# Two heads to a quarter of the weighing's output, and the last two chunks' experts chosen from the first token's value row

## The reference

```
x = x + 0.5 * ffn(layernorm(x))          # silu gate, two gelu layers, 512 wide, ternary weights with scales
x = x + linear_attention(layernorm(x))
x = x + 0.5 * ffn(layernorm(x))          # the same weights
x = x + 0.5 * experts(layernorm(x))      # 8 experts of rank 64, 2 chosen per sequence
x = x + attention(layernorm(x))          # 16 heads of 8, rotary positions, causal, softmax
x = x + 0.5 * experts(layernorm(x))
```

## Time and profile before

| | |
|---|---|
| median of 3 runs | 667.73 us (667.33 to 671.45) |
| the profiled execution | 668.1 us, span 666.3 us |
| PE busy | 631.2 us (95%) |
| PEld busy | 475.8 us (71%) |
| DVE busy | 495.0 us (74%) |
| ACT busy | 495.1 us (74%) |
| POOL busy | 298.8 us (45%) |
| PE in the chain that ended last | 66% |
| DVE in it | 17% |
| ACT in it | 9% |

### The profile page before, as it was taken

How to read it: one execution, slowest core, us unless ns; L and a number is a source line. 1 busy time by engine, 2 the same in 40 slices (tenths; PEclk the granted TensorE clock), 3 DMA queues, 4 the chain that set the end, 5 groups by cost and what they waited for, 6 DMA issues and landing times.

```text
span 666.3 us, 14363 instructions
## 1 busy us (share of the span) xinstructions
PE 631.2 (95%) x5343; PEld 475.8 (71%) x5343; DVE 495.0 (74%) x1300; ACT 495.1 (74%) x846; POOL 298.8 (45%) x461
## 2 busy tenths in 40 slices
PE   4899999999999999999999999989999999999995
PEld 3587878888887878887778887655555666666664
DVE  6767566585586686686798667999898898888655
ACT  5799688788888788787788677337777777777870
POOL 1402111330331535231574563767878745655661
PEclk9999999999999999999999999989999999999999
DMA  9200000000000002000011144442434322221001
GB/s 301 89 0 1 1 0 1 1 0 1 1 0 1 0 18 79 1 1 1 0 49 48 49 139 177 143 144 78 144 123 137 95 93 94 74 72 40 20 9 41
DMA packets 41886, 37.80 MB, mean 57 GB/s; under 512 B 2940, under 2 KB 37020, under 8 KB 41816
## 3 DMA queue, kind: packets, MB, share of 16 engines
q1 hardware_dynamic: 41816, 36.87, 17.6%
HBM read 21.92 MB, written 14.68 MB: 55 GB/s over the span
## 4 chain that ended last, share of the span: by engine, by line
PE 66%; DVE 17%; ACT 9%; issue 5%; POOL 1%; DMA 0%; DVEq 0%; ACTq 0%; POOLq 0%
PE PSA L940 19%; PE PSA L944 19%; PE PSA L1142 6%; DVE MX L1334 5%; PE PSA L959 3%; DVE G L1206 3%; PE PSA L1095 2%; PE PSA L1129 2%; PE PSA L1079 2%; ACT PSA L1380 2%; PE PSA L1072 2%; PE PSA L1151 1%; ACT G L1376 1%; DVE RA L1327 1%; PE PSA L1102 1%
## 5 line engine op out<-in xcount | busy, mean ns | idle before, releaser
L940 PE MATMUL PSA<-ah,WH 128*128 128x512 f32 x320 | 130.0, 406 | 1.5 <-DVE al L1211 0.9
L1334 DVE TENSOR_REDUCE MX<-PSA 128x6 f32<-128x768 f32 x128 | 118.3, 949 | 15.7 <-PE PSA L1102 15.1
L1380 ACT ACTIVATE PSA<-PSA,SC 128x512 f32<-128x512 f32 x128 | 84.7, 662 | 55.0 <-PE PSA L944 54.3
L944 PE MATMUL PSA<-al,WH 128*128 128x512 f32 x320 | 125.2, 391 | 0.0
L1469 ACT ACTIVATE PB<-PSA 128x768 f32<-128x768 f32 x128 | 99.0, 813 | 17.9 <-PE PSA L1129 16.8
L940 PE MATMUL PSA<-bh,WH 128*128 128x512 f32 x256 | 104.8, 409 | 2.7 <-DVE G L1206 2.3
L1552 POOL TENSOR_SCALAR_AFFINE_SELECT PB<-PB 128x512 f32<-128x512 f32 x128 | 79.5, 635 | 51.7 <-ACT PB L1469 50.3
L944 PE MATMUL PSA<-bl,WH 128*128 128x512 f32 x256 | 100.3, 392 | 0.0
L1498 POOL TENSOR_SCALAR VE<-MV 128x4 f32<-128x4 f32 x46 | 10.9, 236 | 194.7 <-DVE MV L1181 194.7
L1211 DVE TENSOR_TENSOR al<-PSA,ah 128x512 fp32r<-128x512 f32 x64 | 44.0, 687 | 52.6 <-ACT ah L1387 52.2
L940 PEld LDWEIGHTS PSA<-ah,WH 128*128 128x128 f32 x320 | 60.2, 188 | 14.8 <-DVE al L1211 2.2
(11 more groups left out here) (148 smaller groups left out, 1321.0 us busy)
## 6 DMA issues: line engine op xcount, KB each, us to landing
KS<-dk SPq DMA_DIRECT2D x32, 192.0 KB
QS<-dq SPq DMA_DIRECT2D x32, 192.0 KB
dk<-CB SPq DMA_DIRECT2D x16, 192.0 KB, 2.3
dq<-CB SPq DMA_DIRECT2D x16, 192.0 KB, 2.3
VA<-in_ones SPq DMA_DIRECT2D x5, 512.0 KB, 4.4
X<-in_x SPq DMA_DIRECT2D x8, 256.0 KB, 6.9
dk<-CB SPq DMA_DIRECT2D x16, 128.0 KB, 1.9
dq<-CB SPq DMA_DIRECT2D x16, 128.0 KB, 1.9
```

What stands on the lines that cost most here:

```text
L940: e.matmul(o, WH[:, col:col + 128], hi, start=first, stop=False)
L944: return e.matmul(o, WH[:, col:col + 128], low, start=False, stop=last)
L1334: e.tensor_reduce(MX[:, u % 2, 1:4, :].rearrange("p t (l g) -> p l t g", l=2)[:, :, :, g], PSA[:, b:b + 2, 0:384].rearrange("p l (t k) -> ...
L1380: e.activation(bank(b), bank(b), ACT.Gelu, scale=SC[:, k:k + 1]).then_inc(a_gelu, 1)
```

## The change

It has two parts, and the planner's costs and priorities are written anew with them.

**Two heads to a quarter.** A head's tile in VA now has 32 columns of which 16 are its own: 8 of values, 8 of ones, and zeros in the other 16. Heads come in pairs, and a second head's columns are the other 16. The first four heads (`weigh`, g even) and the next four (`weighed`, g odd) go into the same bank, the second adding to the first, so that a quarter holds two heads. The bank is held from the one to the other. ScalarE copies it once, after the second; OT has two parts and not four. One `upright` step of four transposes puts the whole unit into a bank, with one reciprocal of 32 sums and one product of 128x256. The heads are ordered anew in the weights, and the table of ones has zeros in it.

**Experts chosen ahead.** For chunks 6 and 7 a new job, `lone`, follows `prepare` once both feed-forward streams are done. It takes the value row of the first token of both units (`lone`), multiplies it by the output weights and adds the token as it stands in X (`lone_x`), subtracts the mean (`lone_m`), and computes logits and the sum of squares (`lone_g`); VectorE picks the two largest of each unit; GpSimd takes the inverse root (`lone_power`), VectorE scales the difference (`lone_df`), and `tanh`, `gate`, `pick` and `pick_b` follow as for the other chunks, the picks not before the second pass of eight (chunk 6) or ten (chunk 7) units. `half_logit`, `half_tanh` and `half_pick` are gone; `half_expert` waits for its own transposed tokens and for GpSimd's sums. The last two chunks' `proj` waits in the planner until `lone_x` has read the token.

The rest: a unit's `peak` waits in the planner until the one before has sent its maxima; the weighing has priority 6.5; what is left out below are waits, counts of semaphores and names of tiles.

```diff
-TILES = {"pass1": "h", "pass2": "h", "weigh": "q"}
+TILES = {"pass1": "h", "pass2": "h", "weigh": "q", "weighed": "q", "max_out": "q"}
...
-WEIGH = 5.9
+WEIGH = 6.5
...
+LONE = 4.0
...
+        if c >= NC - 2:
+            self.add(LONE, self.lone(c, x, xt))
...
+    def lone(self, c, x, xt):
...
+        while len(self.dead) < 2:
+            yield
+        sr, i, mm = self.sr, c - NC + 4, xt
+        for name in ("lone", "lone_x", "lone_m", "lone_g"):
+            yield from self.until(mm.done)
+            b, free = yield from sr.get(self)
+            mm = self.put(name, c=c, x=x, i=i, b=b, emptied=free, src=mm)
+            sr.free[b] = [mm]
+            if name == "lone_x":
+                self.added.add(c)
+        lg = mm
+        for name in ("lone_power", "lone_df", "tanh", "gate"):
+            yield from self.until(mm.done - 0.3)
+            mm = self.put(name, c=c, i=i, src=mm)
+        while self.turn["probs"] < 2 * c - 4:
+            yield
+        self.picked[c] = [self.put("pick", c=c, i=i, src=mm, given=lg), self.put("pick_b", c=c, i=i, src=mm)]
...
+        while self.hmfree is None:
+            yield
         pk = self.put("peak", u=u, src=p1, emptied=self.hmfree)
+        self.hmfree = None
...
-            while self.otfree[u % 2] is None:
+            if g % 2 == 0:
+                while self.otfree[u % 2] is None:
+                    yield
+                b, free = yield from self.sr.get(self)
+                w = self.put("weigh", u=u, g=g, b=b, emptied=free)
+            else:
+                w = self.put("weighed", u=u, g=g, b=b, emptied2=self.otfree[u % 2], src=w)
+                self.otfree[u % 2] = [] if g < 3 else None
+                self.sr.free[b] = [w]
+            self.pbfree[2 * g % SLOTS] = self.pbfree[(2 * g + 1) % SLOTS] = [w]
+            if g < 3:
                 yield
-            b, free = yield from self.sr.get(self)
-            w = self.put("weigh", u=u, g=g, b=b, emptied=free, emptied2=self.otfree[u % 2])
-            self.otfree[u % 2] = [] if g < 3 else None
-            self.sr.free[b] = [w]
-            self.pbfree[2 * g % SLOTS] = self.pbfree[(2 * g + 1) % SLOTS] = [w]
...
-        out, vqfree, self.vqfree[u % 2] = [], self.vqfree[u % 2], None
-        for h in range(2):
-            b, free = yield from self.sr.get(self)
-            o = self.put("upright", u=u, h=h, b=b, emptied=free, emptied2=vqfree, src=w)
-            self.sr.free[b] = [o]
-            out.append(o)
+        vqfree, self.vqfree[u % 2] = self.vqfree[u % 2], None
+        b, free = yield from self.sr.get(self)
+        o = self.put("upright", u=u, b=b, emptied=free, emptied2=vqfree, src=w)
+        self.sr.free[b] = [o]
...
         yield from self.until(on.done)
+        while u // 2 >= NC - 2 and u // 2 not in self.added:
+            yield
...
-        lg = self.put("half_logit", c=c, u=u, x=x, i=n, b=b, emptied=free, emptied2=nfree, src=xt)
-        self.sr.free[b] = [lg]
-        yield from self.until(lg.done - 0.3)
-        gt = self.put("half_tanh", c=c, u=u, i=n, src=lg)
-        yield from self.until(gt.done - 0.3)
-        pk = self.put("half_pick", c=c, u=u, i=n, src=gt, given=lg)
+        while c not in self.picked:
...
+        pk = self.picked[c][u % 2]
         yield from self.until(pk.done)
         b, free = yield from self.sr.get(self)
...
-        self.sr.free[b] = self.xtr.free[x] = self.moer.free[n] = [o]
+        o = self.put("half_expert", c=c, u=u, i=pk.i, h=u % 2, x=x, b=b, emptied=free, src=(pk, xt))
+        self.sr.free[b] = self.xtr.free[x] = [o]
...
-                elif st.name == "half_logit":
...
-                    e.matmul(PSA[:, b, 0:8], XT[:, st.x, 0:1].to_broadcast([128, 128]), WR[:, :], start=True,
-                             stop=True).then_inc(p_half_logit, 1)
                 elif st.name == "half_expert":
-                    w.wait_ge(v_half_wb, n + 1)
+                    w.wait_ge(a_half_xt, st.src[1].n + 1)
+                    w.wait_ge(g_wb, 4 * st.src[0].n + 2 * st.h + 2)
...
                         t = e.matmul(PSA[:, b, 128 * k:128 * k + 128], XT[:, st.x, 128 * k:128 * k + 128],
-                                     WB[:, st.i, 1, :], start=True, stop=True)
+                                     summed(st.i, st.h), start=True, stop=True)
...
+                elif st.name == "lone":
...
+                    e.matmul(PSA[:, b, 0:2], WQ[:, 2, :], XP[:, st.x, 0::256], start=True, stop=True).then_inc(p_lone, 1)
+                elif st.name == "lone_x":
...
+                    e.matmul(PSA[:, b, 0:2], WO[:, :], LV[:, k, :], start=True, stop=False, skip_group_check=True)
+                    for h in range(2):
+                        t = e.matmul(PSA[:, b, h:h + 1], X[:, 4 * c + 2 * h, :], IDN[:, 0:1], start=False, stop=True,
+                                     skip_group_check=True)
...
+                elif st.name == "lone_m":
...
+                    e.matmul(PSA[:, b, 0:2], MEAN[:, 0:1].to_broadcast([128, 128]), LX[:, st.i - 2, :], start=True,
+                             stop=True).then_inc(p_lone_m, 1)
+                elif st.name == "lone_g":
...
+                    for h in range(2):
+                        C = LC[:, st.i - 2, h:h + 1]
+                        e.matmul(PSA[:, b, 16 * h:16 * h + 8], C.to_broadcast([128, 128]), WR[:, :], start=True, stop=True)
+                        t = e.matmul(PSA[:, b, 16 * h + 8:16 * h + 9], C.to_broadcast([128, 128]), C, start=True, stop=True)
...
-                elif st.name == "weigh":
...
+                elif st.name in ("weigh", "weighed"):
+
+                    V, a = VA[u % KEPT], g % 2
...
                     for k in range(2):
                         for v in range(4):
                             P = PB[:, (2 * g + v // 2) % SLOTS, :, v % 2, :]
-                            t = e.matmul(PSA[32 * v:32 * v + 32, b, 128 * k:256], V[:, k, 4 * g + v, :],
-                                         P[:, 1, :] if k else P[:, 0::2, :], start=(k == 0), stop=(k == 1))
+                            t = e.matmul(PSA[32 * v:32 * v + 32, b, 128 * k:256], V[:, k, 8 * (g // 2) + 2 * v + a, :],
+                                         P[:, 1, :] if k else P[:, 0::2, :], start=(k == 0 and a == 0),
+                                         stop=(k == 1 and a == 1), skip_group_check=True)
...
                     for q in range(4):
-                        t = e.transpose(PSA[:, b, 128 * q:128 * q + 128], OT[u % 2][:, q, 128 * st.h:128 * st.h + 128],
-                                        IDN[:, :])
+                        t = e.transpose(PSA[:, b, 128 * q:128 * q + 128],
+                                        OT[u % 2][:, q % 2, 128 * (q // 2):128 * (q // 2) + 128], IDN[:, :])
...
-                elif st.name == "half_logit":
...
-                    e.max(TOP[:, i, 0, :], PSA[:, b, 0:8]).then_inc(v_half_top, 1)
...
-                    e.tensor_tensor(DF[:, i, 0:1], TOP[:, i, 0, 0:1], TOP[:, i, 0, 1:2], ALU.subtract).then_inc(
-                        v_half_df, 1)
-                    e.max_index(WHO[:, i, 0, :], TOP[:, i, 0, :], PSA[:, b, 0:8]).then_inc(v_half_who, 1)
-                elif st.name == "half_pick":
...
-                    who = nc.values_load_multi_w_load_instructions(
-                        WHO[0:1, i, 0, 0:2], (mybir.EngineType.DVE,), min_val=0, max_val=7)[1]
...
+                elif st.name == "lone_m":
...
+                    e.tensor_tensor(LC[:, i - 2, :], LX[:, i - 2, :], PSA[:, b, 0:2], ALU.subtract).then_inc(v_lone, 1)
+                elif st.name == "lone_g":
...
+                    for h in range(2):
+                        e.max(TOP[:, i, h, :], PSA[:, b, 16 * h:16 * h + 8]).then_inc(v_lone_top, 1)
+                    e.tensor_scalar(LE[:, i - 2, :], PSA[:, b, 8:25:16], 1.0 / 128, EPS, ALU.mult, ALU.add).then_inc(
+                        v_lone_df, 1)
...
+                        e.max_index(WHO[:, i, h, :], TOP[:, i, h, :], PSA[:, b, 16 * h:16 * h + 8]).then_inc(v_lone_who, 1)
...
+                    e.tensor_copy(BOTH[:, i, :, :], WHO[0:1, i, :, 0:2]).then_inc(v_lone_both, 1)
+                    e.tensor_tensor(DF[:, i, :], TOP[:, i, :, 0], TOP[:, i, :, 1], ALU.subtract).then_inc(v_lone_df, 1)
+                elif st.name == "lone_df":
...
+                    e.tensor_tensor(DF[:, i, :], DF[:, i, :], LR[:, i - 2, :], ALU.mult).then_inc(v_lone_scaled, 1)
...
-                    O = bank(b).rearrange("p (m r) -> p m r", r=32)
+                    O = bank(b).rearrange("p (m r) -> p m r", r=16)
...
-                    e.reciprocal(RC[:, st.h, :], O[:, :, 8]).then_inc(v_rc, 1)
...
+                    e.reciprocal(RC[:, u % 2, :], O[:, :, 8]).then_inc(v_rc, 1)
...
-                    e.tensor_tensor(VQ[:, u % 2, st.h, :].rearrange("p (m r) -> p m r", r=8), O[:, :, 0:8],
-                                    RC[:, st.h, :].rearrange("p (m o) -> p m o", o=1).to_broadcast([128, NH, 8]),
```

(32 more changed lines are left out.)

122 lines of the change are left out of this document (68 added, 54 removed), and 12 rows, old and new, of the table TAKES.

## The result

The changed kernel took **661.11 us** (median of 6 runs, 659.31 to 662.67) against 669.77 us (667.33 to 671.45) for the kernel before, run beside it: a ratio of 0.9872 (95% interval 0.9844 to 0.9901), 8.6 us less. The forecast was 658.5, the range 651.5 to 664.5. The profiled execution took 659.31 us with a span of 657.2, against 668.1 and 666.3: 9.1 us of span.

What follows compares the result with a forecast made beforehand. It took TensorE and VectorE to share the bound in the bulk, ScalarE joining from 620 us, then a chain of short steps. Terms -6.2 - 0.35 - 1.6 - 1.0 = -9.15 gave 658.5 us, range 651.5 to 664.5.

Steps and rivals of the forecast that it cites:

- Part 1, the end: After the last unit's projection: logit, tanh and choice leave the chain and VectorE's queue; -6.2 us, ends -6.7 and -3.
- the 5.05: Last unit, projection's end to last addition: remaining steps 4.55 us plus ten hops 0.5, before half of unit 14's steps.
- TensorE's +5.1: Bulk: small fp32 matmuls for choosing chunks 6 and 7 ahead add 5.1 us on TensorE.
- Part 2, the upright step: Last unit on VectorE: one reciprocal and product pair in place of two; -0.35 us, ends 0 and -0.5.
- Part 3, the last exponentials: Stage 620 to 646 us: fewer ScalarE copies and TensorE transposes, savings not adding; -1.6 us, ends -0.5 and -2.5.
- Part 4, the bulk: Bulk before 620 us: upright savings nearly cancelled by steps choosing ahead, TensorE -1.0, VectorE -0.2; taken as -1.0 us.
- the order at nothing: Bulk: the step order laid anew by changed priorities and costs was priced at zero, with -3 to +4 in the range.
- The small matmuls: Bulk, TensorE: choosing-ahead matmuls priced from the trace at 0.13 to 0.15 us a record, 36 records.
- A: Bulk gives part back through GpSimd's picks, late selects and small matmuls: bulk +4 us, total 663.5 us; 27%.
- B: Bulk gains in full, 6.1 us, small steps falling into TensorE's idle time; total 652.1 us; 20%.
- C: Weighing's shared bank held too long between halves, 3.3 us a pair, costing TensorE time; total 681 us; 5%.
- D: The end doesn't shrink because another wait is as long; -3 in all, 664.7 us; 3%.

Runs made afterwards that it cites:

- held_best: held_short with the maximum's way out no longer counted as a quarter tile in the planner; 653.72 us.
- chosen_only: Kernel before plus only the choosing ahead of experts for chunks 6 and 7, with weighing, uprights and priorities as before; 666.66 us, ratio 0.998.
- order_only: Kernel before with only the planner's order settings (weighing priority 6.5, maxima as quarter tile, peak's wait), no work changed; 669.11 us, ratio 1.0024.
- heads_only: Kernel before plus only two heads to a quarter and the new order settings, experts chosen as before; 661.15 us, ratio 0.9893.
- held_late: held_short with the weighing's priority at 7.0 for 6.5; 664.42 us.
- order_late: Changed kernel with the weighing's priority at 7.0 for 6.5, nothing else; 659.85 us.
- held_short: Changed kernel, but a weighing's first half is put only when the exponentials of both halves are there; 657.51 us.
- lone_twice: Changed kernel with every small matmul of the choosing-ahead steps issued twice, 36 more records, same order; 668.74 us.

## Why the prediction was right, and where not

**Part 1, the end: -6.2 forecast, -5.3 measured.** The chain was the right one. What was mis-sized is what lands in it: I let in 0.5 us of unit 14's steps; it was 1.3, and they were chunk 5's second addition, unit 13's norm and unit 13's last addition, which I had not looked for. In held_best, where nothing stands there, it is the 5.05 that was written down. The price of the move is in chosen_only: -1.3 for the part as a whole, and the prediction's terms for it, -6.2 and TensorE's +5.1, make -1.1.

**Part 2, the upright step: -0.35 forecast, +0.5 measured**, outside its ends. The reciprocal of 32 sums takes 345 ns, not 0.27; and what decides between the last exponential and the last projection is not this pair but how two units pass each other: unit 15's transposes (644.37) came behind those of unit 14's `flat`, which waited for VectorE's product until 644.04.

**Part 3, the last exponentials: -1.6 forecast, -3.2 measured**, beyond the end of -2.5. I held that the savings of ScalarE and TensorE don't add. Doubled, five copies cost 2.0 us of this stage and eight transposes 0.9, together 2.9, so they do. Not all of the -3.2 need be work, though: in order_only, with nothing saved, the stage is 1.3 us shorter than before, and in heads_only, with the same settings, 3.2.

**Part 4, the bulk: -1.0 forecast, -1.1 measured, right in part by luck.** Two large terms do cancel, as forecast: up to the last maximum heads_only gains 7.2 us, where the forecast had 6.1 (twelve times 0.5 is 6.0), and chosen_only loses 6.2, where it had 5.1. But they aren't made as written. order_only gains 5.4 of the 7.2 with no work saved, and by the same settings the two heads to a quarter bring 1.8 more. The copies, which the forecast gave nothing here, cost 3.1 us when they are doubled. So "the order at nothing" is the step of the working that fails: in total time the settings alone are worth +1.6 us in one kernel and -3.2 in the other, and two of them move the same work over 10.7 us. The range had -3 to +4 for it; the centre had luck.

The small matmuls were priced well: eight records of the logits start at 505.66 and end at 506.71, 0.13 us each, and their doubling at a full clock costs 2 to 5 us. The Trainium skill, TensorEngine Tiling (Array Packing), section Instruction Overhead, gives about 60 cycles for a matmul of one column, an estimated 0.9 us for all 36 records, against 4.7 by this row: the trace doesn't agree with it for these fp32 matmuls.

**The rivals.** A (the bulk gives back, 663.5) is true in that the choice is paid for ahead of the end, which the sum hides: choosing ahead puts the last projection 4.4 us later in chosen_only, and 6.1 later in the changed kernel than in heads_only. That it was GpSimd's picks isn't shown. B (full gain, 652.1) didn't come with this order; another order of the same work reaches 653.7, and one with half of the choosing ahead 654.3. C (the bank held) falls by its size, 1.2 us a pair and not 3.3, and no gain belongs to the hold. D is false: the end did shrink.

What stays open: which steps in the list make held_best quicker than held_late. The planner's plan tells orders apart without a chip to some extent: measured medians lie 11.5 to 15.7 us above `P` in every row that has a plan of its own. That is enough to choose between orders whose `P` are 6 us apart, not between closer ones: order_late and held_short have 644.2 and 644.5, and took 659.85 and 657.51.

**The better version** is held_best: 653.72 us, 14.4 less than the kernel before and, by the ratios, 0.9% below the changed kernel (0.5 to 1.3, from the two intervals).

## What to carry to other kernels

When the engines run a list laid out by a planner, an edit has two effects, its work and the order that comes of it, and the second was as large as the first here (10.7 us between orders of the same steps): lay the list under several settings before judging an edit, and count fillers as idle time. A gain in the bulk can vanish in a queue at the end (order_only), so compare the stages and not only the times. A step moved out of the end is paid for where it goes (-5.8 there and +4.4 before it in chosen_only; -9.0 and +6.1 from heads_only to the changed kernel). For the last unit's chain, list every instruction on its engines that becomes ready at the same time, from other chunks too.

## What was not expected of the hardware

TensorE's granted clock fell in lone_twice while the engine is shown as busy. Of the 28 records from 530.64 to 533.46 us, 16 have one or two columns; the clock is 0.67 from 532.5 us, 0.50 from 535 to 542.5, and rises when scores and weighing have returned. A record of the logits takes 0.21 us there instead of 0.13. In the changed kernel, with half as many small ones, the clock reads 1.00 in the windows from 500 to 620 us. That these records made it fall is what the order in time suggests; one profile isn't a proof: another run of the same kernel with the same records has a mean clock of 0.999 over its whole span, so they don't always bring such a fall. And an earlier fall in the profiled run has another thing before it. There TensorE had waited 1.8 us for the transfer that brings the maxima back (timeline of lone_twice, then its windows):

```profile
488.61 0.34 PE L1203 MATMUL PSA<-QS,KS 52*128 52x256 bf16 x4 [1.83 <-DMA QS<-MT]
...
485.00:490.00 5.00, 3.17 (x54) 1.70 (x46) 2.63 (x4) 2.42 (x5) 2.42 (x5) 0.90 0.48 132
490.00:495.00 5.00, 4.92 (x47) 2.25 (x39) 3.12 (x7) 2.40 (x5) 1.27 (x3) 0.76 0.37 113
```

What such a fall goes with can be read from the runs of one kernel. Between a mean clock of 0.999 and one of 0.984 lone_twice goes from 663.08 to 672.88 us, and order_late from 656.0 at 1.00 to 665.4 at 0.984: about 1.5% of time for 1.5% of clock. Smaller differences of the mean show nothing so regular (held_short took 657.5 us at 0.994 and 657.7 at 1.00). Where the clocks of two kernels' runs differ by a per cent, look at them before calling a few microseconds the order's.
